# A six-stage block on one core: stages that run into one another, two accumulators for the routed experts

## The reference

```
x = ln(x + spectral(x))            # FFT filter, 24-bit code correction
x = ln(x + gated cross attention with ctx)
x = ln(x + mixture(x))             # 8 experts, each with 512 given tokens:
    gathered = x[tok[e]]; h = gelu(gathered @ W1[e] + b1[e]); out = h @ W2[e] + b2[e]
    result[tok[e]] += out * combine[tok[e], e]
x = ln(x + self attention)         # 16 heads of 16, rotary positions over all 256 features
x = ln(x + cross attention(x, ctx))  # 16 heads of 64
x = ln(x + routed(x))              # top 8 of 32 experts, at most 256 tokens each, F = 192
    topw, topi = top_k(softmax(x @ gate), 8); topw /= sum(topw)
    pos = place of the token in its expert's list, those from 256 on are dropped
    out[token] = sum over its experts of topw * (silu(x @ Wg[e]) * (x @ Wu[e])) @ Wd[e]
```

## Time and profile before

| | us |
|---|---|
| runs | 2322.5, 2326.05, 2320.73 |
| the profiled execution, its time | 2315.22 |
| its span | 2313.3 |
| busy: PE, DVE, ACT, POOL | 1738.0, 1236.0, 1020.0, 1009.3 |
| mean granted TensorE clock | 0.879 of 2.4 GHz |
| stages, from the timeline: gated ends | 376.5 |
| mixture's last scatter issued | 655.6 |
| self-attention from, to | 680.8, 1180 |
| cross-attention from, to | 1180, 1938 |
| router, then experts from, to | 1938, 2050, 2288 |
| last norm ends | 2313.3 |

### The profile page before, as it was taken

How to read it: one execution, slowest core, us unless ns; L and a number is a source line. 1 busy time by engine, 2 the same in 40 slices (tenths; PEclk the granted TensorE clock), 3 DMA queues, 4 the chain that set the end, 5 groups by cost and what they waited for, 6 DMA issues and landing times. The chain is left out here.

```text
span 2313.3 us, 23934 instructions
## 1 busy us (share of the span) xinstructions
PE 1738.0 (75%) x7497; PEld 1256.8 (54%) x7497; DVE 1236.0 (53%) x2315; ACT 1020.0 (44%) x1920; POOL 1009.3 (44%) x838
## 2 busy tenths in 40 slices
PE   5588882799914887778938888889889885478881
PEld 2266672677712565556626566556556554356560
DVE  5455562566534797978735555555555651722222
ACT  1054441455400585758825656556555661011120
POOL 0000000334241475758824555555554660357773
PEclk9699996899965799999969999999999996689995
DMA  1100004344223532323020110110100103037674
GB/s 44 31 34 10 1 1 167 113 111 113 59 77 72 93 51 61 56 56 56 1 85 22 35 26 21 37 25 21 38 24 24 26 26 113 1 82 164 155 167 95
DMA packets 88421, 138.38 MB, mean 60 GB/s; under 512 B 19728, under 2 KB 54974, under 8 KB 85480
## 3 DMA queue, kind: packets, MB, share of 16 engines
q1 hardware_dynamic: 61744, 99.13, 16.5%
q0 software_dynamic: 19184, 29.59, 6.8%
q10 hardware_dynamic: 7368, 8.14, 1.1%
HBM read 96.23 MB, written 31.72 MB: 55 GB/s over the span
## 5 line engine op out<-in xcount | busy, mean ns | idle before, releaser
L1961 POOL TENSOR_TENSOR STp_lo_use<-ST_use,STp_hi_use 128x512 fp32r<-128x512 f32 x256 | 335.1, 1317 | 163.4 <-ACT ST_use L1812 158.7
L1526 POOL TENSOR_TENSOR STp_lo<-ST,STp_hi 128x512 fp32r<-128x512 f32 x192 | 257.5, 1359 | 117.3 <-ACT ST L1359 116.2
L1808 ACT ACTIVATE STp_hi_use<-bank 128x512 fp32r<-128x512 f32 x256 | 152.8, 597 | 199.2 <-PE bank L1758 196.7
L1355 ACT ACTIVATE STp_hi<-bank 128x512 fp32r<-128x512 f32 x256 | 159.6, 624 | 73.2 <-PE bank L1293 72.6
L1427 DVE TENSOR_REDUCE nmax<-bank 128x1 f32<-128x512 f32 x256 | 168.7, 681 | 34.5 <-PE bank L1282 34.1
L1871 DVE TENSOR_REDUCE nmax_use<-bank 128x1 f32<-128x512 f32 x256 | 170.6, 681 | 5.0 <-PE bank L1732 2.3
L1282 PE MATMUL bank<-rows_k,rows_q 96*128 96x512 f32 x256 | 122.6, 487 | 52.0 <-DVE nmax L1427 44.7
L1359 ACT ACTIVATE ST<-bank 128x512 f32<-128x512 f32 x256 | 161.0, 629 | 0.0
L1812 ACT ACTIVATE ST_use<-bank 128x512 f32<-128x512 f32 x256 | 151.8, 593 | 0.0
L1732 PE MATMUL bank<-ks,qs 128*128 128x512 f32 x256 | 115.9, 454 | 30.3 <-DVE nmax_use L1871 16.2
L2396 POOL DMA_INDIRECT acc_scratch<-res,sidx_all x64 | 101.8, 1591 | 54.9 <-DMA acc_scratch<-res,sidx_all 33.9
(11 more groups left out here) (433 smaller groups left out, 4795.2 us busy)
## 6 DMA issues: line engine op xcount, KB each, us to landing
Wgu<-in_Wgu SPq DMA_DIRECT2D x32, 384.0 KB
stage_use<-in_W SPq DMA_DIRECT2D x8, 1024.0 KB, 4.9
stage<-in_W SPq DMA_DIRECT2D x8, 1024.0 KB, 5.0
rows_q<-hop_scratch SPq DMA_DIRECT2D x64, 128.0 KB, 4.0
rows_k<-hop_scratch SPq DMA_DIRECT2D x64, 128.0 KB, 5.8
ks<-ks SPq DMA_DIRECT2D x64, 128.0 KB, 2.2
rinv<-rinv_scratch SPq DMA_DIRECT2D x64, 128.0 KB, 2.8
hop_scratch<-qkp_hi SPq DMA_DIRECT2D x8, 512.0 KB, 2.9
```

The costliest lines, as they stand in the source:

```text
L1355: A.activation(STp[u % NHI][0], bk.ap, ACT.Exp)
L1526: G.tensor_tensor(STp[u % NHI][1], ST[u % NFULL], plain(STp[u % NHI][0]), ALU.subtract).then_inc(low["pool"].sem, low["pool"].inc(u))
L1808: A.activation(STp[u % NHI][0], bk.ap, ACT.Exp)
L1961: G.tensor_tensor(STp[u % NHI][1], ST[u % NFULL], plain(STp[u % NHI][0]), ALU.subtract).then_inc(low["pool"].sem, low["pool"].inc(u))
```

## The change

1. `program` has no barrier of its own any more; `spectral`, `gated`, `self_heads` and `cross_heads` end with one, `mixture` and `routed` with none over all engines. `gated` writes each normed quarter to `rows_scratch` and to the accumulator, from SyncE, and loads the token indices; `tok_row` is loaded per expert. Ahead of `self_heads` only PE, ACT, DVE and SP meet, once the last but one expert's scatters have landed. The norm of the mixture is in `self_heads`.
2. `self_heads`: memsets of `rows_q` and `rows_k` shrink to one row, `Vone`'s goes to GpSimd; for the first batch each stack and value tile has a PSUM bank of its own, hops go out per half, and two DMAs fill a quarter of `rows_q` or `rows_k`.
3. `cross_heads`: second head of a pair one step earlier, output products of the second half later, norm offsets +2, memsets gone, products over 65 rows and not 96.
4. Router: selection per batch; the sums over earlier tiles are 15 matmuls; slots carry the token number alone and go to DRAM and back per group; weights are 32 more columns of `tokens_scratch` and come with the gathered rows; the product with the token number is on ACT; tables are fp32r and 128 columns wide.
5. Experts: two accumulators in turn, for even and odd experts, each with its own semaphore; an expert's scatters stand before the gathers of the expert five ahead; `norm_sums` adds the second accumulator.

The core of the diff:

```diff
-        self.tokens_d = nc.dram_tensor("tokens_scratch", (B * S, D), f32, kind="Internal").ap()
-        self.acc_d = nc.dram_tensor("acc_scratch", (B * S + CAP, D), f32, kind="Internal").ap()
+        self.tokens_d = nc.dram_tensor("tokens_scratch", (B * S, D + E1), f32, kind="Internal").ap()
+        self.acc_d = [nc.dram_tensor("acc_scratch%d" % z, (B * S + CAP, D), f32, kind="Internal").ap() for z in range(2)]
...
             stage(kit)
-            nc.all_engine_barrier()
...
                 V.wait_ge(sums_in[k].sem, sums_in[k][name])
+                if other is not None:
+                    V.wait_ge(others_in[k].sem, others_in[k][k])
+                    V.tensor_tensor(X[:, quarter[k], :], X[:, quarter[k], :], other[:, quarter[k], :], ALU.add).then_inc(added.sem, added.inc(k))
...
         def pool():
-            G.dma_start(idx, T["idx"]).then_inc(idx_in.sem, idx_in.inc("idx"))
-            G.dma_start(rows_d[:, D:GW], T["combine"]).then_inc(combine_in.sem, combine_in.inc("combine"))
-            G.dma_start(acc_d[0:B * S].rearrange("(t p) d -> p t d", p=P), X).then_inc(acc_in.sem, acc_in.inc("acc"))
-            G.dma_start(tok_row, bass.AP(T["tok"].tensor, 0, [[0, P], [1, E0 * C0]])).then_inc(tok_in.sem, tok_in.inc("tok"))
...
-            G.wait_ge(stored.sem, stored[E0 - 1, CT0 - 1])
...
-        nc.all_engine_barrier()
-    norm_sums(kit, "s3")
+        for engine in (PE, A, V, SP):
+            engine.wait_ge(stored.sem, stored[E0 - 2, CT0 - 1])
+        nc.multi_engine_barrier([PE.engine, A.engine, V.engine, SP.engine])
...
+        def norm_loads(engine, quarters):
+            engine.wait_ge(kit.stored0.sem, kit.stored0[E0 - 1, CT0 - 1])
+            for k in quarters:
+                engine.dma_start(X[:, quarter[k], :], tiles_d[:, quarter[k], :]).then_inc(kit.quarter_in[k].sem, kit.quarter_in[k].inc("s3"))
...
+                if of_next(s, 38) == 0:
+                    norm(1)
+                    average(2)
+                    norm(2)
+                    average(3)
+                    norm(3)
...
         def pool():
-            for rows in (rows_q, rows_k):
-                m = G.memset(plain(rows[MAX_ROW:ROWS]), 0.0)
-            m.then_inc(g_own.sem, g_own.inc("rows zero"))
-            G.wait_ge(g_own.sem, g_own["rows zero"])
-            G.memset(plain(rows_k[MAX_ROW:MAX_ROW + 1]), 1.0).then_inc(zeroed.sem, zeroed.inc("rows"))
+            G.memset(plain(rows_k[MAX_ROW:ROWS]), 1.0).then_inc(zeroed.sem, zeroed.inc("rows"))
             G.wait_ge(zeroed.sem, zeroed["rows"])
+            G.memset(plain(Vone), 0.0).then_inc(g_own.sem, g_own.inc("s4 V"))
...
+            root(0)
+            root(1)
...
-        OUTS = ((50, 0, 0), (58, 0, 1), (STEPS + 18, 1, 0), (STEPS + 24, 1, 1))
+        OUTS = ((50, 0, 0), (58, 0, 1), (STEPS + 24, 1, 0), (STEPS + 25, 1, 1))
...
-                for r, of, half in ((3, "q", 0), (5, "k", 0), (7, "q", 1), (7, "k", 1)):
+                for r, of, half in ((3, "q", 0), (5, "k", 0), (6, "q", 1), (6, "k", 1)):
...
-                for t in range(NT):
-                    PE.matmul(bank[0].ap[:, t * E1:(t + 1) * E1], tri[:, 0, :], marks16[:, t, :], start=True, stop=False)
-                    m = PE.matmul(bank[0].ap[:, t * E1:(t + 1) * E1], tri[:, 1, :], before16[:, t, :], start=False, stop=True)
+                PE.matmul(bank[0].ap, tri[:, 0, :], marks16.rearrange("p t e -> p (t e)"), start=True, stop=False)
+                for t in range(NT - 1):
+                    to_later = bass.AP(marks16.tensor, marks16.offset + t * E1, [marks16.ap[0], [0, NT - 1 - t], [1, E1]])
+                    m = PE.matmul(bank[0].ap[:, (t + 1) * E1:], tri[:, 1, :], to_later, start=False, stop=t == NT - 2)
...
+                for g in range(4):
+                    z = g % 2
+                    A.wait_ge(hot_b.sem, hot_b[g])
...
+                    for t in range(NT):
+                        m = A.activation(BV[z][:, t, :], B_[z][:, t, :, :].rearrange("p e j -> p (e j)"), ACT.Copy, scale=token1[:, t:t + 1])
...
+            G.wait_ge(rows_in.sem, rows_in["weight"])
             for e in range(RB - 1):
                 gather(e)
-            G.wait_ge(own.sem, own["sidx"])
+            G.wait_ge(acc_in.sem, acc_in["zeros"])
             for e in range(E1):
+                bk = bank[6 + e % 2]
+                G.wait_ge(bk.free, bk.free_at["down1", e])
+                if e % 8 == 0:
+                    G.wait_ge(own.sem, own["sidx", e // 8])
+                if e > 1:
+                    G.wait_ge(stored[e % 2].sem, stored[e % 2][e - 2, CT1 - 1])
+                for t in range(CT1):
+                    n = e * CT1 + t
+                    G.indirect_dma_start(acc_d[e % 2], bass.IndirectOffsetOnAxis(ap=sidx[:, n:n + 1], axis=0), res[e % 2][:, t, :], None,
+                                         compute_op=ALU.add).then_inc(stored[e % 2].sem, stored[e % 2].inc((e, t)))
                 if e + RB - 1 < E1:
                     gather(e + RB - 1)
-                bk = bank[6 + e % 2]
-                G.wait_ge(bk.free, bk.free_at["down1", e])
-                if e:
-                    G.wait_ge(stored.sem, stored[e - 1, CT1 - 1])
-                for t in range(CT1):
-                    n = e * CT1 + t
-                    G.indirect_dma_start(acc_d, bass.IndirectOffsetOnAxis(ap=sidx[:, n:n + 1], axis=0), res[e % 2][:, t, :], None,
-                                         compute_op=ALU.add).then_inc(stored.sem, stored.inc((e, t)))
-            G.wait_ge(stored.sem, stored[E1 - 1, CT1 - 1])
...
-    norm_sums(kit, "s6", kit.out)
+    norm_sums(kit, "s6", acc_d, stored, kit.out)
```

More of the change, by code:

```diff
@@ L1405, in act, with average @@
                         A.activation(attT[:, c, :], SPARE.ap, ACT.Copy).then_inc(SPARE.free, 1)
+        def average(k):
+            V.wait_ge(kit.quarter_in[k].sem, kit.quarter_in[k]["s3"])
+            for t in range(NT)[quarter[k]]:
+                m = V.bn_stats(all_stats[:, t, :], X[:, t, :])
+            m.then_inc(own.sem, own.inc(("s3 stats", k)))
+            V.wait_ge(own.sem, own["s3 stats", k])
+            for t in range(NT)[quarter[k]]:
+                m = V.bn_aggr(all_mv[:, t, :], all_stats[:, t, :])
+            m.then_inc(averaged.sem, averaged.inc(("s3", k)))
@@ new lines, in root, with norm @@
+        def root(k):
+            G.wait_ge(averaged.sem, averaged["s3", k])
+            G.tensor_scalar(all_veps[:, quarter[k]], all_mv[:, quarter[k], 1], EPS, None, ALU.add).then_inc(g_own.sem, g_own.inc(("s3 veps", k)))
+            G.wait_ge(g_own.sem, g_own["s3 veps", k])
+            G.tensor_tensor(all_rstd[:, quarter[k]], all_veps[:, quarter[k]], mhalf[:, quarter[k]], ALU.pow).then_inc(rooted.sem, rooted.inc(("s3", k)))
+        def norm(k):
+            V.wait_ge(rooted.sem, rooted["s3", k])
+            for t in range(NT)[quarter[k]]:
+                m = V.tensor_scalar(X[:, t, :], X[:, t, :], all_mv[:, t, 0:1], all_rstd[:, t:t + 1], ALU.subtract, ALU.mult)
+            m.then_inc(normed.sem, normed.inc(k))
@@ new lines, in all_hopped, with stack_rows @@
+        def all_hopped(engine, b, n):
+            for g in range(DC):
+                engine.wait_ge(hopped[n][g].sem, hopped[n][g][b, len(HOPS[n]) - 1])
+        def stack_rows(engine, b, i, n):
+            hs = slice(i * HS, (i + 1) * HS)
+            for k in range(2):
+                first = k * n * HD
+                engine.dma_start(plain((rows_q, rows_k)[n][2 * k * HD:2 * (k + 1) * HD, hs]), hop_d[b % 2, n, hs, first:first + 2 * HD].rearrange("h f s -> f h s")).then_inc(stacked[i].sem, stacked[i].step)
@@ L2128, in pe, with slot_table @@
                         m.then_inc(bk.full, 1)
+                def slot_table(g):
+                    PE.wait_ge(slots_in.sem, slots_in[g])
+                    PE.wait_ge(bank[3].free, bank[3].use(("table", g)))
+                    PE.transpose(bank[3].ap[:, 0:16], slot_rows[:, g, :], ident[0:16, 0:16]).then_inc(bank[3].full, 1)
+                PE.wait_ge(kit.tables_in.sem, table)
+                turn(0)
+                for b in range(B):
+                    if b + 1 < B:
+                        turn(b + 1)
                     lbk = bank[2 + 4 * (b % 2)]
@@ L2162, in act @@
                 for b in range(B):
[L2163 to L2169 removed]
+                    bk = bank[4 * (b % 2)]
@@ L2186, in dve, with choose @@
+                agree(3)
+                addresses(2)
+                addresses(3)
+            def choose(b):
+                lbk = bank[2 + 4 * (b % 2)]
+                V.wait_ge(lbk.full, lbk.full_at["logits", b])
+                V.tensor_copy(L[:, of(b), :].rearrange("p t e -> p (t e)"), lbk.ap[:, 0:TB * E1]).then_inc(lbk.free, 1)
+                V.wait_ge(lbk.free, lbk.free_at["logits", b])
+                for t in range(NT)[of(b)]:
                     m = V.max(top[:, t, :], L[:, t, :])
-                m.then_inc(own.sem, own.inc("top"))
```

460 lines of the change are left out of this document (248 added, 212 removed).

## The result

The changed kernel takes 2396.05 us as the median of four runs (2381.6, 2391.7, 2400.4 and 3412.8), against 2322.45 for the kernel before. Without the fourth, a slow run for which no cause is on record, it is 1.0294 times as long, 95% interval 1.0242 to 1.0347. The forecast was 2165, so the change went the other way. The profiled execution took 2391.7 us with a span of 2390.4 and a mean granted TensorE clock of 0.817, before 0.879.

The account below looks back on a forecast made before the run. No engine was taken to bound the whole kernel: time was a sum of seams, TensorE's cross-attention stalls and GpSimd's expert pace. Terms −22−36+2−36−41−27+2=−158 took the median 2322.5 to about 2165 us, range 2128 to 2206.

Parts of the forecast that it names:

- Self-attention loop: Self-attention loop: fewer row and hop DMAs, but ACT waits for more, smaller hops; +2 us, ends 0 and +6.
- Rival (d): Cross-attention heads: new gaps drop TensorE's granted clock to 0.5; 2405 us if at half the time; chance 0.03.
- Seam 1: Gated layer to mixture: first gather and first expert matmul come earlier; −22 us, ends −17 and −26.
- Mixture: Mixture's first product to its last scatter: no change forecast, 0 us.
- Seam 2: Mixture to self-attention: −27 us from last scatter to first xT, −9 from there to first score product; −36 in all.
- Cross-attention: Cross-attention heads: earlier split of the second head, later output products remove TensorE's stalls; −36 us, ends nothing and −52.
- waits under 0.5: Cross-attention heads: the second head's row-max transpose would wait under 0.5 us.
- Router: Router: selection per batch, matmuls for the GpSimd chain, cheaper tables; −41 us, ends −35 and −46.
- Experts: Routed expert loop: two accumulators remove scatter waits, −17 us, and the last five scatter pairs −10; −27, ends −14 and −38.
- Final norm: Final norm: one barrier less against more loads and additions; +2 us, ends −2 and +8.

Follow-up runs that it names:

- e15: The kernel before with both self-attention score products over 65 rows instead of 96: 2326.18 us, ratio 1.0028.
- e14: The kernel before with only self-attention's row-maximum products over 64 rows, the other score products staying at 96: 2471.61 us, ratio 1.0663.
- e12: The changed kernel with self-attention's row-maximum products over 65 rows instead of 64, row 64 of rows_q zeroed by DMA: 2195.59 us, ratio 0.9472.
- e3: The kernel before with self-attention's maximum products over 64 rows and its other score products over 65: 2512.26 us, the middle of two runs.
- e1: The changed kernel with both self-attention score products over 96 rows again, the extra rows zeroed: 2207.45 us, ratio 0.9516.
- e11: e1 with the zeroing of the extra rows on DVE instead of GpSimd and later stacks of k in self-attention: 2198.03 us, ratio 0.9465.
- e13: e12 with stacks of k 3 and 2 steps later for all batches but the first, and gather ahead of the scatters: 2175.3 us, ratio 0.9385.
- e7: e1 with the cross-attention heads' second head split at step 7 again instead of 6: 2244.7 us.
- e10: e1 with GpSimd's old order among the experts, gather for the expert five ahead before the scatters: 2200.61 us.
- e9: e1 with two accumulators, but each expert's scatters waiting for those of the expert right before: 2234.39 us.

## Why the prediction was wrong

The step that failed is "Self-attention loop: +2, ends 0 and +6". I counted its DMAs and waits and passed over the one edit in it that changes TensorE's products, `ROWS` from 96 to 65 and, in the maximum products, `rows_q[0:MAX_ROW]`: 64 rows. The description of the change and the core of the diff leave it out too. So a term that measured some 195 us stood at nothing, without a reason in the text. I had taken fewer rows for free, because in the kernel before the 96-row and the 128-row products both take 0.39 us at the full clock. It is free from 96 to 65 (e15, 1.0028). At 64 the body is longer by 157 (e14 against the kernel before), 193 (changed kernel against e12) or 211 (e3 against e15), and the time by 154, some 200 and 186. Rival (d) named the clock, but in the cross-attention heads. There it rose from 0.94 to 0.97, and all maximum products of that stage have 128 rows. The other terms gained most of what was forecast, and this one ate it: see e12 at the end of this section.

The Trainium skill has the rule that I should have weighed (TensorEngine Tiling (Array Packing), "Key Properties", and "Available Configurations" for the modes): changing the tiling mode, not just the tile, drains TensorE; 64 rows is a tiling mode of its own there. If a product over exactly 64 rows runs in that mode, the edit makes two changes of mode a step. The trace agrees: two weight loads a step, the 64-row one and the next, have 0.65 and 0.44 of idle ahead of them, and of the row counts that were run (64, 65, 80, 96, 128) only 64 costs anything. The mode itself is in no trace. The page gives no price; here it is 0.39 us a step at the full clock (1.32 for 0.93) and 0.58 at half (2.29 for 1.71).

That the lower level of the clock goes with it is shown (0.63 with 64 rows, 0.92 with 65, same schedule). Why it does not come back isn't shown by any run, and stays open: the gaps and the 64-row products themselves come and go together in all of them.

The other steps, by their numbers (the +6.3 ahead of them is in stages that do nearly the same work; the first mixture product lies anywhere from 401.6 to 412.6 in the profiles of e1 to e12 that share all of it):
- **Seam 1** −18 for −22: the gather came 3.9 us after its write was issued, as thought (386.72), but the first weights, two DMAs of 1 MB, took 12 and 15 us with everything else in flight. The prediction counted 5 for the first, the time for one alone.
- **Mixture** +4.9 for 0: the last scatter waits 7.48 instead of 2.98 for the one before, while self-attention's weight loads run beside it (issued at 636.83, 637.51 and 641.79). The cover that I gave those loads probably had this price; no run moves them away.
- **Seam 2** −28 for −27 to xT, and −3.6 for −9 after it: with 10 DMAs of hops and 16 row loads on two queues, the four loads that the first product needs had landed only at 708.1; TensorE waited 20.0 for rows instead of 6.9. The memsets weren't slowed (6.93 beside DVE's statistics), as the prediction said. Its reading of the earlier trace rows is a mean of two: the trace has DVE's two L1441 at 0.69 and 1.75, so the first ran as fast as L1449 does alone and the second was held.
- **Self-attention loop**, apart from the rows: +20 for +2 (e1 437.0, before 416.5). Later stacks of k took 19 of it away in e11 and again in e13 (419.6 for e12's 438.6), and with them most of ACT's waits for hops, three of up to 5.3 us in the changed kernel.
- **Cross-attention** −42 for −36; the split alone 37 (e7). The sign "waits under 0.5" didn't come: it is 1.01 each, and the number is near all the same, because the waits for the other maxima went from 16.2 to 10.4 where the prediction let them grow.
- **Router** −44 for −41. Expert 0's transposes start 70.5 us behind the router's start, forecast 71.
- **Experts** −24 for −27. GpSimd is busy 139 of 172 us, and its waits for earlier scatters are 1.2 us in 4 times, for 18.9 in 12. 27 scatter pairs start 6.4 apart each, as forecast; the last four gaps take 19.1 together, where 4.4 each was forecast. The new order gave 5 of the gain away (e10). The prediction's fixed 2.0 us leaves 0.97 of the 2.97 for 128 KB, which no run takes apart; that a second accumulator hides the wait is shown by e9.
- **Final norm** +3.8 for +2: the first quarter's loads from both accumulators took 8.3 us with 4 MB in flight, for 4.97.

With 65 rows for 64 the change measures as e12: 2195.6 for 2318.1, −122 for −158, inside the range that was given. Of the 36 that are missing, the self-attention loop's own +20 is the largest part.

## What to carry to other kernels

When a diff changes the number of rows of a TensorE product, check whether it goes from above 64 to 64, and price the step in which products of both kinds alternate, not the product. Here one more row, of zeros, bought back 8% of the kernel's time; other row counts up to 64 were not run. And go through a list of edits by engine: an engine that a stage has as its near-bound (here 348 of 416 us) deserves the question for every edit that touches it, even one that only makes its work smaller.

## What the runs showed of the hardware

- A product over 64 rows between products over 65 to 128: its weight load and the next one lose their overlap, 0.39 us a pair at the full clock; 65, 80, 96 and 128 rows alternate with 128 at no cost (bodies 433.6 to 438.6). With 64 rows the granted clock of the stretch is 0.63, with 65 rows 0.92.
- Sixty-four columns of weights are no such case: in the cross-attention heads of the changed kernel L1871 (128*64) stands between products with 65 columns and takes 396 ns, as they do (400 and 396).
- A DVE TENSOR_SCALAR of 128x2 took 6.97 us beside a GpSimd memset of 6.92 (e11, above), and 0.16 in the changed kernel with none beside it:

```profile
648.64 0.16 DVE L1508 TENSOR_SCALAR bq_use<-bqkv 128x2 f32<-128x2 f32 x1
```

The trace of the kernel before has it too, and it could have been read there: beside the memset that runs from 694.66 to 701.58, the same operation takes 1.55 us and ends with it, at 701.60.

```profile
700.05 1.55 DVE L1417 TENSOR_SCALAR bq_use<-bqkv 128x2 f32<-128x2 f32 x1
```

So a memset on GpSimd, which reads nothing, does hold up DVE for that kind of operation. The prediction asked only whether DVE slows memsets. Statistics (BATCH_NORM_STATS2) beside a memset weren't held: 1.41 for four at 656.42 in the changed kernel, with the memset of `Vone` running from 655.99. The four in e11 that show 6.90 stand in DVE's line behind the held operation and end with it, at 670.74. The Trainium skill (SBUF — State Buffer, "Who interferes with whom") names tensor_scalar among the operations that can take both ports and contend with GpSimd, and says that a DVE instruction with at most one SBUF input outside these modes doesn't. The trace agrees: 6.97 for 0.16, and the statistics at 1.41.
